# Cross-attention and mixture feed-forward: the batch loop shifted, scores and values of one batch walked beside the next batch's cross-attention

## The reference, cut to what matters

```python
x = x + xattn(layernorm(x), ctx)               # softmax over 64 context rows
z = layernorm(x)
q, k, v = z @ wq, z @ wk, z @ wv               # 16 heads of 16
scores = where(causal, q k^T / sqrt(16), min)
o = softmax(scores) @ v                        # 512 x 512 a head
h = z + rmsnorm(o @ wo, attn_norm_w)
dense = h + rmsnorm((silu(h @ w1) * (h @ w3)) @ w2, ff_norm_w)
probs = softmax(z @ router_w)                  # 8 experts, top 2
sparse = rmsnorm(sum of the top 2 experts' outputs, moe_norm_w)
out = x + dense + sparse
```

## Time and profile before

| | |
|---|---|
| median of three runs | 1718.03 us (1711.98 to 1718.67) |
| the profiled execution | 1725.52 us, its span 1723.7 us |
| PE busy | 1407.8 us, 82% of the span |
| DVE busy | 845.5 us, 49% |
| ACT busy | 543.7 us, 32% |
| POOL busy | 503.4 us, 29% |
| granted TensorE clock, mean | 0.914 of full speed |

### The profile page before, as it was taken

The page is one execution under the profiler, slowest core; times in us unless marked ns, Lnnn a source line. Parts: engine busy times, 40 slices in busy tenths (PEclk is TensorE's granted clock), DMA queues, the critical chain, the costliest instruction groups (busy, mean ns, idle before and its releaser), DMA issues.

```text
span 1723.7 us, 25491 instructions
## 1 busy us (share of the span) xinstructions
PE 1407.8 (82%) x7721; PEld 955.2 (55%) x7722; DVE 845.5 (49%) x1877; ACT 543.7 (32%) x1018; POOL 503.4 (29%) x680
## 2 busy tenths in 40 slices
PE   7765896899788978897889789878978789999930
PEld 3542565567555755675467556655655465666620
DVE  0445463646464546545555556454636423333347
ACT  3230532152225214430532053215321413333322
POOL 3123043204411340323032303330432013555532
PEclk9885999899889989998999889989997889999975
DMA  5314105010501050014102310401040352222247
GB/s 215 127 49 87 26 1 125 10 38 0 131 4 37 2 129 19 21 35 99 38 1 61 74 38 0 105 30 38 1 122 13 114 87 68 85 85 85 86 165 256
DMA packets 107072, 116.68 MB, mean 68 GB/s; under 512 B 39416, under 2 KB 80912, under 8 KB 107024
## 3 DMA queue, kind: packets, MB, share of 16 engines
q1 hardware_dynamic: 88080, 98.10, 20.3%
q0 software_dynamic: 8576, 17.87, 3.3%
q10 hardware_dynamic: 10368, 0.04, 0.3%
HBM read 71.36 MB, written 44.21 MB: 67 GB/s over the span
## 4 chain that ended last, share of the span: by engine, by line
PE 56%; issue 19%; DMA 7%; POOL 5%; DVE 5%; SPq 4%; ACT 3%; ACTq 0%; POOLq 0%; DVEq 0%
PE ps L892 9%; PE ps L925 7%; PE ps L763 6%; DMA room<-parts_d 5%; PE ps L746 5%; PE ps L900 5%; PE ps L775 3%; PE ps L942 3%; PE ps L813 3%; SPq L436 3%; PE ps L715 2%; PE ps L877 2%; PE ps L734 2%; PE ps L668 2%; PE ps L687 2%
## 5 line engine op out<-in xcount | busy, mean ns | idle before, releaser
L813 PE MATMUL ps<-room 96*128 96x128 bf16 (+3 forms) x512 | 151.2, 353 | 118.3 <-DMA room<-parts_d 88.1
L892 PE MATMUL ps<-hT,w 128*128 128x512 f32 x768 | 205.6, 418 | 9.7 <-DVE gT L1406 8.3
L1055 ACT ACTIVATE room<-ps 128x1024 f32<-128x1024 f32 x160 | 159.5, 1023 | 143.5 <-PE ps L847 140.0
L1355 DVE TENSOR_REDUCE nm<-ps 128x2 f32<-128x256 f32 (+3 forms) x160 | 127.0, 823 | 104.7 <-PE ps L814 101.8
L892 PEld LDWEIGHTS ps<-hT,w 128*128 128x128 f32 x768 | 148.1, 196 | 47.0 <-DVE gT L1406 9.0
L813 PEld LDWEIGHTS ps<-room 96*128 96x128 bf16 x512 | 55.0, 108 | 180.7 <-issue 119.3
L1077 ACT ACTIVATE th<-ps 128x512 f32<-128x512 f32 x64 | 38.3, 598 | 364.5 <-PE ps L892 364.5
L925 PE MATMUL ps<-room 128*128 x288 | 137.2, 599 | 3.5 <-ACT room L1092 3.5
L845 PE MATMUL ps<-room 99*128 99x512 bf16 (+3 forms) x512 | 127.0, 323 | 8.9 <-DMA room<-mT 6.3
L900 PE MATMUL ps<-w,gT 128*128 128x256 f32 x512 | 121.4, 380 | 0.4 <-DVE gT L1406 0.4
L562 POOL TENSOR_TENSOR ve_a<-mv,eps 128x1 f32<-128x1 f32 (+1 forms) x40 | 9.9, 247 | 376.5 <-DVE mv L1240 247.7
(11 more groups left out here) (216 smaller groups left out, 2554.7 us busy)
## 6 DMA issues: line engine op xcount, KB each, us to landing
room<-parts_d SPq DMA_DIRECT2D x96, 256.0 KB, 7.0
room<-xs_d SPq DMA_DIRECT2D x72, 128.0 KB, 2.0
room<-pair_d SPq DMA_DIRECT2D x8, 1024.0 KB, 7.5
room<-in_L_ffn_ew SPq DMA_DIRECT2D x24, 256.0 KB, 6.2
xin<-in_x SPq DMA_DIRECT2D x8, 512.0 KB, 4.0
parts_d<-xnT SPq DMA_DIRECT2D x32, 128.0 KB, 1.8
parts_d<-o_tok SPq DMA_DIRECT2D x32, 128.0 KB, 1.8
parts_d<-oT SPq DMA_DIRECT2D x32, 128.0 KB, 1.7
```

The source lines that it names most:

```text
L813: mm(bank(o, n), q_rep[0:KREP, rep_at(h), t * P:n], k_rep[0:KREP, rep_at(h), 0:n], start=True, stop=False)
L892: last = mm(bank(up_banks(b, m)[i]), w[:, x, k, m * P:(m + 1) * P], hT[:, y, k, :], start=((x, y, k) == terms[0]), stop=((x, y, k) == term ...
L1055: done(fn(prob[:, grp % 2, u * 1024:(u + 1) * 1024], ps[:, n % 2 * 1024:n % 2 * 1024 + 1024], ACT.Exp), "b_exp")
L1355: done(v.tensor_reduce(nm[:, t, 2 * hp:2 * hp + 2], pair_ps, AX.X, ALU.max, negate=True), "a_max")
```

## The change

The scores, values and out_t of a batch move into the next iteration. There they belong to c and are dealt, step by step, between the PE steps of batch b's cross-attention, which are cut into smaller ones (m into four, cs, ct and cv into halves). Everything of c's network stands after them, beside qk, v, the routing and the maxima. All 32 maxima steps of a batch now lie in that second half, always a pair of heads at a time, in banks 0 to 3. In fours to sixes they are dealt around fu and fd, and the two DVE operations of fu have become a step of their own, fg. The score units are half as wide (512 columns, 40 a batch, banks 6 and 7 in turn), prob has one buffer in place of two, and a group's value is cut in three chunks. There are two shifts, not three.

On SP, m_row is loaded in the iteration that uses it, behind that batch's context and x loads; y of batch c is still the last thing of an iteration. On POOL the residual of c is kept in a buffer of its own, hb (f_hb), and x1 + xn is taken early (z). In the first batch the split of w1 and w3 (L1039, L1312) comes later, in route, and the replica loads don't wait for it. After the last iteration the zero rows of the expert buffers are written ahead of the expert weights.

```diff
+UNITS = 10
+CHUNKS = 3
+SHIFTS = ((0, 8), (8, 16))
+def scores_of(grp):
+    order = [("sc", grp, u) for u in range(6)] + [("va", grp, 0)]
+    order += [("sc", grp, u) for u in range(6, 9)] + [("va", grp, 1), ("sc", grp, 9)]
+    return order
+SCORES = []
+for _g in range(G):
+    SCORES += scores_of(_g)[:2] if _g else scores_of(0)[:2]
+    SCORES += [("va", _g - 1, 2)] if _g else []
+    SCORES += scores_of(_g)[2:5]
+    SCORES += [("out_t", _g - 1)] if _g else []
+    SCORES += scores_of(_g)[5:]
+SCORES += [("va", G - 1, 2)]
+CROSS = [
+    ("x_turn",), ("m", 0), ("m", 1), ("f_hb",), ("m", 2), ("m", 3), ("bqk", 0), ("bqk", 1),
+    ("cs", 0, 0), ("cs", 0, 1), ("vw", 0), ("vw", 1), ("exp", 0), ("vw", 2), ("vw", 3), ("sum", 0), ("x_bias",),
+    ("cs", 1, 0), ("cs", 1, 1), ("exp", 1), ("sum", 1), ("ct", 0, 0), ("ct", 0, 1),
+    ("cs", 2, 0), ("cs", 2, 1), ("exp", 2), ("cv", 0, 0), ("cv", 0, 1), ("sum", 2), ("ct", 1, 0), ("ct", 1, 1),
+    ("cs", 3, 0), ("cs", 3, 1), ("exp", 3), ("cv", 1, 0), ("cv", 1, 1), ("sum", 3), ("ct", 2, 0), ("ct", 2, 1),
+    ("cv", 2, 0), ("cv", 2, 1), ("ct", 3, 0), ("ct", 3, 1), ("cv", 3, 0), ("cv", 3, 1), ("norm_3",),
 ]
+ON_PE = ("x_turn", "m", "bqk", "cs", "vw", "ct", "cv")
+def interleaved():
+    first, rest = SCORES[:6], SCORES[6:]
+    slots = [i for i, s in enumerate(CROSS) if s[0] in ON_PE and s[:2] != ("cv", 3)]
+    order, given = [("x_norm",)] + first, 0
+    for i, s in enumerate(CROSS):
+        order.append(s)
+        if i in slots:
+            want = (slots.index(i) + 1) * len(rest) // len(slots)
+            order += rest[given:want]
+            given = want
+    return order
+STEPS = interleaved() + [
+    ("out_t", G - 1), ("f_o_turn",), ("x2_turn",), ("f_wo",), ("qk", 0), ("qk", 1), ("f_o_norm",), ("qk", 2), ("qk", 3),
+    ("v", 0), ("v", 1), ("v", 2), ("v", 3), ("route", 0), ("f_h_turn",), ("route", 1), ("fu", 0), ("f_yb",), ("route", 2),
+    ("fg", 0), ("fu", 1), ("fg", 1), ("fd", 0), ("slots",), ("fu", 2), ("fg", 2), ("scatter",), ("fd", 1),
+]
+_max = [("max", hp, t) for hp in range(H // 2) for t in range(T)]
+for _m in range(3, FB):
+    STEPS += [("fu", _m)] + ([("shift", 0)] if _m == 6 else []) + [_max[0], ("fg", _m), _max[1], ("fd", _m - 1)] + _max[2:5]
+    _max = _max[5:]
+    if _m == 5:
+        STEPS += _max[:1] + [("shift_parts", 0)]
+        _max = _max[1:]
+STEPS += [("fd", FB - 1)] + _max[:2]
+_max = _max[2:]
+STEPS += [
+    ("f_end",), *_max[:2], ("f_scale",), *_max[2:], ("z",), ("shift_parts", 1), ("shift", 1),
+]
...
+def up_banks(b, m):
+    return ((0, 1) if b is None else (2, 3)) if m % 2 and (b is None or m < 3) else (4, 5)
...
             def batch(b, c):
                 if b is not None:
-                    if c is not None:
-                        before(sp, b, "rep_k")
-                        sp.sem_inc(reps_free, 1)
                     before(sp, b, "vw_ps")
...
+                if c is not None:
+                    for i, (first_head, end_head) in enumerate(SHIFTS):
+                        need(sp, c, "mT_sb", i + 1)
+                        for r in range(MROWS):
+                            done(sp.dma_start(q_rep[KREP + r:KREP + r + 1, rep_at(first_head):rep_at(end_head - 1) + 1:KD, :],
+                                              mT[r * H + first_head:r * H + end_head, i, :]), f"m_row{i}", 16)
...
-                        if c is None:
-                            sp.wait_ge(p0["split"], 2)
...
                 if c is not None:
                     need(sp, c, "y", 1)
-                    done(sp.dma_start(at_batch(y_d, c), yb[:, :, :]), "y_out", 16)
+                    done(sp.dma_start(at_batch(y_d, c), hb[:, :, :]), "y_out", 16)
...
+                    elif kind == "sc":
                         grp, u = step[1:]
+                        n = grp * UNITS + u
+                        need(act, c, "b_ps", n + 1)
+                        if grp and u in (0, 4, 8):
+                            need(act, c, "va_ps", (grp - 1) * CHUNKS + u // 4 + 1)
+                        done(fn(prob[:, u * 512:(u + 1) * 512], bank(6 + n % 2), ACT.Exp), "b_exp")
```

More of the change, by code:

```diff
@@ L78 @@
[L78 to L89, removed]
@@ new lines, in batch @@
+                        for a in range(4):
+                            pa = i * 4 + a
+                            last = mm(bank(i, P, a * P), bq_bc[:, pa, :], k_bd[:, pa, :], start=True, stop=True)
+                        done(last, "bqk_ps")
+                    elif kind == "vw":
+                        i = step[1]
+                        if i < 2:
+                            need(pe, b, ("m_act", "m_dve")[i], 2)
+                        else:
+                            need(pe, b, "vw_sb", i - 1)
+                        for a in range(2):
+                            last = mm(bank(2 + i % 2, D, a * D), v_bd[:, 2 * i + a, :], wo_c[:, 2 * i + a, :], start=True, stop=True)
+                        done(last, "vw_ps")
@@ new lines, in batch @@
+                        if half == 0:
+                            need(pe, b, "sc_nrm", t + 1)
+                            if t == 0:
+                                need(pe, b, "vw_sb", 4)
+                        elif t:
+                            need(pe, b, "x1", t)
+                        for a in range(4):
+                            last = tr(bank(2 + half, P, a * P), s_sb[:, t % 2, (half * 4 + a) * P:(half * 4 + a + 1) * P], ident[:, :])
+                        done(last, "pT_ps")
@@ new lines, in batch @@
+                        n = grp * UNITS + u
+                        if n == 0:
+                            before(pe, c, "fd_n")
+                        if u == 0 and grp in (0, 2):
+                            need(pe, c, f"m_row{grp // 2}", 48)
+                        if n >= 2:
+                            need(pe, c, "b_exp", n - 1)
+                        for j, kb, at in score_rows(u):
+                            o = (6 + n % 2) * 512 + at
+                            h = rep_at(4 * grp + j)
+                            mm(ps[:, o:o + S - kb * P], k_rep[0:KREP + MROWS, h, kb * P:(kb + 1) * P], q_rep[0:KREP + MROWS, h, kb * P:S],
+                               start=True, stop=False, skip_group_check=True)
+                            last = mm(ps[:, o:o + P], ident_b[:, :], mask_kq[:, :], start=False, stop=True, skip_group_check=True)
@@ new lines, in batch @@
+                        done(last, "b_ps")
+                    elif kind == "va":
+                        grp, chunk = step[1:]
+                        need(pe, c, "b_exp", grp * UNITS + (4, 8, 10)[chunk])
+                        if grp and chunk == 0:
+                            need(pe, c, "av_sb", grp)
+                        for kb in ((0,), (1, 3), (2,))[chunk]:
+                            for j in range(4):
+                                at, w = prob_at(j, kb), S - kb * P
+                                last = mm(ps[32 * j:32 * j + 32, 4 * 512 + kb * P:5 * 512], v_aug[:, v_at(kb, 4 * grp + j):v_at(kb, 4 * grp + j) + 32],
+                                          prob[:, at:at + w], start=(kb == 0), stop=(kb == 2), skip_group_check=True, tile_position=(0, 32 * j))
+                        done(last, "va_ps")
+                    elif kind == "out_t":
@@ L865, in batch @@
-                        done(last, "av_ps")
-                    elif kind == "out_t":
-                        out_t(b, step[1])
-                    elif kind == "f_out_t":
-                        out_t(c, step[1])
+                            need(pe, c, "o_nrm", grp)
+                        for t in range(T):
+                            last = tr(bank(5, P, t * P), av[:, t * P:(t + 1) * P], ident[:, :])
+                        done(last, "avT_ps")
                     elif kind == "f_o_turn":
-                        before(pe, c, "fd_n")
+                        need(pe, c, "b_exp", per["b_exp"])
```

602 lines of the change are left out of this document (266 added, 336 removed), and 3 rows, old and new, of the table STEPS.

## The result

The changed kernel takes 1785.15 us, median of four runs (1784.3 to 1793.1), against 1716.94 for the kernel before beside it: a ratio of 1.041, 95% interval 1.038 to 1.045. The profiled execution has a span of 1782.5 us against 1723.7, so 58.8 us are to be found.

What follows compares the result with a forecast made beforehand. PE was taken as the bound, with some 131 us of work in 165.1, the rest waits and low clock. Stages and clock sum to 168.1 us an iteration; with the ends, 1718.0 + 5.7 = 1724 us, eight in ten 1692 to 1750.

Steps and rivals of the forecast that it cites:

- slowest rival: Clock stays at 1.2 GHz after x_turn and falls again at the 2.85 us stall: 1747 us, chance 0.35.
- (a): From x_turn to f_o_turn: 62.1 us of PE work plus 4.4 and 3.4 of waits, 69.9 us.
- (b): f_o_turn, x2_turn and wo: 5.3 us.
- (c): From the end of wo to the first max, held by the replica loads: 32.0 us, 5.5 of it idle.
- (d): From the first max to the end of fd 7, where DVE's order costs: 38.1 us.
- (e): From fd 7 to the next x_turn, a new wait with x loaded only behind y: 21.1 us.
- clock: Slow work after the mostly idle PE stretch between fd 7 and x_turn: 1.7 us lost an iteration.
- first rival: Clock low for the first 10 us after x_turn, falling again at the 2.85 us stall: 1747 us, chance 0.35.
- the old rate: At 0.51 us a maximum, first max to the end of fd 7 would take 35.6 us.
- The ends: First max at 139.5, loop's first x_turn at 182.8; last batch's scores alone, its f_o_turn at 1380.0, then 3 us less.

Runs made afterwards that it cites:

- e3: Changed kernel with exp 1 and its sum moved behind the transposes of cross-attention tile 0: 1758.73 us, ratio 1.019 to the kernel before.
- e7: Changed kernel with the edits of e1 and e3, plus six score units computed at the end of their batch's own iteration: ratio 1.014 to the kernel before.
- e8: The kernel of e7 run again, on another chip: 1720.53 us, ratio 1.001 to the kernel before.
- e2: Changed kernel with the dealing undone, all scores and values in one block ahead of cross-attention: 1837.27 us, ratio 1.065 to the kernel before.
- e1: Changed kernel with the next batch's x and context and this batch's m rows loaded ahead of y: 1783.87 us, ratio 1.035 to the kernel before.
- e6b: Changed kernel with fg and fd first, then five maxima together, in every round; second run: 1804.21 us, ratio 1.050 to the kernel before.
- e4: Changed kernel with 20 and 22 unused matmuls put on PE in the boundary's two waits: 1823.05 us, ratio 1.059 to the kernel before.
- e9: Kernel of e7 with DVE's norm of x ahead of the second shift's copy and y ahead of the second m rows: 1714.93 us, ratio 0.998 to kernel before.
- e10b: Kernel of e9 with the last group's output between the halves of cv 3, second run: 1700.60 us, ratio 0.988 to the kernel before.
- e11: Changed kernel with only the edits of e1 and e3 together: 1757.87 us, ratio 1.021 to the kernel before.
- e9b: The kernel of e9 run again: 1714.30 us, ratio 0.995 to the kernel before.
- e5: Changed kernel with POOL's addition z waiting until the second shift is copied out: ratio 1.064 to the kernel before, which took 1774 us in that sitting.
- e6: Changed kernel with fg and fd first, then five maxima together, in every round; first run: ratio 1.073 to the kernel before.
- e10: Kernel of e9 with the last group's output between the halves of cv 3, first run: ratio 1.005 to the kernel before, which took 1764 us.
- e5b: The kernel of e5 run again: 1797.21 us, ratio 1.043 to the kernel before.

## Why the prediction was wrong

The mechanism, a shorter first iteration given back by longer later ones, is what happened; the size was not, and 1785 lies above the forecast of 1724 and above the slowest rival, 1747. The first iteration gained 28 us (23 predicted), the six longer ones lost 6 x (175.6 - 165.1) = 63 (18 predicted), and the rest, from the eighth x_turn on, lost 551 - 527 = 24 (11 predicted; it holds one more such iteration).

By stages, of the iteration at 704.38, predicted and measured: (a) 69.9 and 77.0; (b) 5.3 and 7.1; (c) 32.0 and 30.3; (d) 38.1 and 38.8; (e) 21.1 and 23.3; clock 1.7, inside the others. In all 168.1 and 176.5.

**Two terms of the sum failed, by some 5 us each: the clock, and the work of (a).** The other errors come to -1.6 together, since shorter waits in (a) and an earlier (c) make up for (d) and (e); that is luck.

**The clock.** I put one fall at the boundary and 1.7 us for it. In (a) to (c) of this iteration PE was busy at 0.5 for 3.1 us at the start of (a), 3.4 behind the 2.39 us stall, 3.4 in (b) and 3.4 in (c). Half of each is lost: 1.6 + 1.7 + 1.7 + 1.7 = 6.7, so 5.0 more than the term. An iteration in which the stall opens no spell has 4.1 us at the start of (a) and loses 5.5; over six iterations the mean is 6.0. The rows bear out the halving roughly: (b) took 7.1 us with its spell and 5.5 without one in e3.

Part of that is the first rival's mechanism, "falls again at the 2.85 us stall", given 0.35. But the rival put 10 slow us at the start of (a), where there were 3 to 5, and the spells in (b) and (c) stood in neither. On (c) I wrote that it idles too little for a fall; behind its wait of 1.90 us the clock fell in every iteration. I also took 3 us of slow work behind 630.67 for the price of a long stop; the trace of before has the clock at 0.5 until 634.80, 4.1 us. e3 shows the parts at the stall and in (b); the others are read from windows, and the spell at the start of (a) went only with e7's whole edit, in four of e8's seven iterations.

The Trainium skill, TensorE: Matmul & The Clock Gate, section HAM oscillation, says that repeated idle gaps keep taking the clock down. I had weighed it and set it below my forecast. The trace agrees in direction, three or four falls an iteration, but not wait by wait: behind the same 2.39 us stall the clock fell in three iterations of seven.

**(a), the work.** Its walk through the exponentials held: a stall of 2.85 predicted and 2.39 found, at the end 3.3 and 2.90, and idle time in all 6.6 where 7.8 was in the sum. The work did not: PE was busy 70.4 us, less 3.3 for the clock 67.1, where I had 62.1. From the rows, four groups of values cost 10.3 in place of 9.2, 34 score units about 11.7 in place of 10.5, cs and cv some 1.4 more by their dealt halves (1.77 to 1.93 for 1.72), m, bqk and vw some 0.8 more (m 0.95 a quarter for 0.89), the transposes of out_t 0.5. I had costed cut steps at the merged rate. e2 shows the price of cutting for cs and m; for the rest that it is the cutting is argued.

**(e), the transfers.** y was there after 7.9 us (8.0), x issued 4.2 later (4.3), but it landed after 5.6, not 4.0, for a reason that no run shows, and from the start of the norm to x_turn it took 5.5, not 4.7, DVE's scaling being 2.23 us beside POOL's copy. That is 2.2 in all. That x is loaded late was right, but not that it alone binds: e1 took it away and won 1.6.

**(c) and (d).** (c) was 1.7 shorter though the clock took 1.7 of it: PE no longer waits for the replica loads in the loop (one wait of 13.7 us, in the first batch). My last issue at 12.85 and trip of 19.2 were too late by 2 us together: measured are 12.3 and 17.6, and the last load lands 0.4 us before the first max, so they all but bind. (d) was right within 0.7, but its comparison with the old rate was not: e6b puts the maxima together and is slower.

**The ends.** x_turn of the second batch was predicted at 182.8 and came at 177.8, because the loads came earlier than I had them: the first max was at 134.1, not 139.5. From there to x_turn it took 43.7 us where I had 43.3. Behind the last f_o_turn 3 us were predicted and 6 came.

## What to carry to other kernels

When steps are merged into one in-order list, look for the one instruction of a second engine that waits in front of the copies that PE needs: moving exp 1 behind ct 0 was worth more than loading x early. Count a stall of two or three us in dense TensorE work at its length and, as a risk, half of the slow time that can follow it or a later wait; read it from windows of several iterations, since the same stall does not open a spell each time. When steps are cut and dealt, don't take the merged rate for the pieces: the sum over a long stage was 5 us of 62 too low. At a boundary with several waits one behind the other, removing one shows the next (behind the late loads the loop's end, behind nparts the norm of x); what pays is independent work carried into the gap, and it pays only if it is work that must be done anyway.

## What the runs showed of the hardware

**DVE beside POOL.** A copy of 128x32 with a cast takes 0.18 us alone and 2.20 while POOL adds 128x1024 (2.39 us); it ended at 867.89 and POOL's addition at 867.86. With the addition moved, all sixteen took 0.181 to 0.183.

**The loop's end.** PE stands 3.1 to 5.1 us on "issue" where the body starts again, at every boundary of e1, e4, e9, e10b and e11 (3.43, 4.24 and 3.73 in single iterations of e1, e4 and e11), in e1, e4 and e11 with a second gap of 1.7 to 3.7 us a few matmuls later. With each of these gaps go two or three transfers on q8, a DMA queue of the kind "instruction". e8 shows it best, for it has the gap at one boundary of six:

```profile
510.62 1.93 PE L900 MATMUL ps<-room,v_aug 128*32 128x512 f32 x8 [3.39 <-issue]
```

DMA queues of e8 from 502 to 512 us, and at a later boundary, from 830 to 845:

```profile
q8 instruction: 3, 0.05, 2.5%
```

```profile
q1 hardware_dynamic: 192, 0.55, 9.7%
q14 instruction: 2, 0.02, 0.3%
```

At its other five boundaries nothing moves on q8 and PE has no such gap. In e9b the first four have both, the last two neither. The kernel before has both at two boundaries, a gap of 2.91 us each (1196.85 in the earlier trace rows), and at the others a single transfer or none, and no gap. The changed kernel and e3 have the transfers at every boundary, under the wait for the late rows. So PE most likely waits for its own instructions there. That is read from traces, no edit tested it, and why the transfers come at some boundaries only stays open.

**Stops in some sittings.** e5, e6, e7 and e10 ran where the kernel before took 1764 to 1774 us in place of 1717 to 1728. DVE then stood idle in front of maxima with nothing of its core to wait for. Waits of DVE in e5_z_apart:

```profile
DVE nm L1380 <- remote: 74.4, 19, 8.8
DVE nm L1380 <- issue: 28.5, 8, 7.7
```

The changed kernel's trace has none of it, nor has e5b, on the same chip at another time. The cause stays open. Only ratios within such a sitting were used, and each of these kernels ran again.
